# Warm-up products, another order of the first norm, roundings and averages at other places, values in groups of four

## What is computed

```python
x = x + L0(_gn(x))      # q, k, v = g @ W + b; softmax(q k^T / 8 + rel_h + rel_w) v; @ Wp + bp
x = x + L1(_gn(x))      # qkv = g @ qkv_w^T; softmax over 49 neighbours; @ out_w^T

def _gn(v, G=32, eps=1e-5):
    g = v.reshape(B_, H_, W_, G, C_ // G)
    m = jnp.mean(g, axis=(1, 2, 4), keepdims=True)
    s = jnp.var(g, axis=(1, 2, 4), keepdims=True)
    return ((g - m) / jnp.sqrt(s + eps)).reshape(v.shape)
```

## Time and profile before

| | us |
|---|---|
| median of 3 runs | 3250.79 |
| lowest and highest | 3249.35, 3253.89 |
| profiled run, its time | 3253.59 |
| its span in the trace | 3251.8 |
| TensorE busy | 3164.5 (97%) |
| VectorE, ScalarE, GpSimd busy | 1731.7, 1228.9, 1085.2 |

### The profile page before, as it was taken

The page is one execution under the profiler, slowest core; times in us unless marked ns, Lnnn a source line. Parts: engine busy times, 40 slices in busy tenths (PEclk is TensorE's granted clock), DMA queues, the critical chain, the costliest instruction groups (busy, mean ns, idle before and its releaser), DMA issues.

```text
span 3251.8 us, 48955 instructions
## 1 busy us (share of the span) xinstructions
PE 3164.5 (97%) x20428; PEld 2368.3 (73%) x20428; DVE 1731.7 (53%) x1889; ACT 1228.9 (38%) x1397; POOL 1085.2 (33%) x618
## 2 busy tenths in 40 slices
PE   8999999999999999999999999999999999999999
PEld 6876658886787665888678756588877876568876
DVE  4447745346434774543644477444473457744435
ACT  2345542224234554213423455321342346532132
POOL 0037770025003776002400477600340047750043
PEclk9999999999999999999999999999999999999999
DMA  3211013113421101311432100121153111022103
GB/s 124 91 36 24 20 45 117 40 53 121 140 99 27 24 20 48 114 40 59 139 134 80 33 21 17 58 104 44 61 165 116 65 34 27 14 88 81 40 24 123
DMA packets 170520, 220.39 MB, mean 68 GB/s; under 512 B 113856, under 2 KB 126400, under 8 KB 170304
## 3 DMA queue, kind: packets, MB, share of 16 engines
q1 hardware_dynamic: 168768, 215.68, 21.2%
q10 hardware_dynamic: 1536, 1.57, 0.2%
HBM read 141.70 MB, written 50.33 MB: 59 GB/s over the span
## 4 chain that ended last, share of the span: by engine, by line
PE 83%; DVE 5%; issue 4%; ACT 3%; SPq 2%; DMA 2%; POOL 1%; ACTq 0%; DVEq 0%; POOLq 0%
PE score L1156 15%; PE score L1157 14%; PE score L1158 14%; PE lot L1313 10%; PE score L1278 9%; PE lot L1228 5%; PE lot L1231 4%; PE score L1285 3%; PE score L1291 3%; SPq L428 2%; DVE recip L931 2%; PE lot L1330 1%; PE lot L1199 1%; PE lot L1261 1%; PE lot L1156 1%
## 5 line engine op out<-in xcount | busy, mean ns | idle before, releaser
L568 POOL TENSOR_TENSOR acc<-acc,prob 128x1024 f32<-128x1024 f32 x288 | 714.9, 2482 | 240.0 <-ACT prob L748 211.3
L748 ACT ACTIVATE prob<-score 128x1024 f32<-128x1024 f32 (+3 forms) x576 | 512.5, 908 | 374.7 <-PE score L1291 296.2
L889 DVE TENSOR_REDUCE max_part<-lot 128x1 f32<-128x512 f32 x640 | 411.1, 684 | 173.4 <-PE lot L1231 173.4
L1313 PE MATMUL lot<-prob,v 128*64 128x512 f32 (+4 forms) x2496 | 470.9, 514 | 7.2 <-ACT o_raw L647 4.4
L1156 PE MATMUL score<-a_hi,w_hi 128*128 128x512 f32 x1152 | 459.1, 399 | 12.9 <-DVE q_lo L1002 5.1
L1157 PE MATMUL score<-a_lo,w_hi 128*128 128x512 f32 x1152 | 450.8, 391 | 0.0
L1158 PE MATMUL score<-a_hi,w_lo 128*128 128x512 f32 x1152 | 450.0, 391 | 0.0
L568 POOL TENSOR_TENSOR acc<-prob 128x1024 f32<-128x1024 f32 x48 | 113.8, 2372 | 860.9 <-ACT prob L748 860.9
L815 DVE TENSOR_TENSOR w_lo<-raw,w_hi 128x1536 fp32r<-128x1536 f32 x95 | 178.8, 1882 | 298.2 <-ACT w_hi L605 297.9
L1156 PE MATMUL score<-w_hi,a_hi 128*128 128x256 f32 x1152 | 336.1, 292 | 0.0
L1313 PEld LDWEIGHTS lot<-prob,v 128*64 128x64 f32 x2496 | 161.5, 136 | 235.9 <-issue 199.1
(11 more groups left out here) (112 smaller groups left out, 5456.5 us busy)
## 6 DMA issues: line engine op xcount, KB each, us to landing
raw<-weights SPq DMA_DIRECT2D x96, 768.0 KB, 4.4
g_mem<-g SPq DMA_DIRECT2D x24, 1024.0 KB, 4.7
xin<-x_t SPq DMA_DIRECT2D x24, 512.0 KB, 6.0
xr<-x_t SPq DMA_DIRECT2D x24, 512.0 KB, 5.0
x_mem<-xr SPq DMA_DIRECT2D x24, 512.0 KB, 6.5
xr<-x_mem SPq DMA_DIRECT2D x24, 512.0 KB, 5.6
y_t<-xr SPq DMA_DIRECT2D x24, 512.0 KB, 6.8
recip<-recip SPq DMA_DIRECT2D x368, 32.0 KB, 1.9
```

What stands on the lines that cost most here:

```text
L568: nc.gpsimd.tensor_tensor(acc[:, :, a:b], with_, now, ALU.add).then_inc(added, 1)
L748: nc.scalar.activation(prob[:, ug % P_SLOTS, :, 0:b - a], score[:, u % 2, :, 0:b - a], ACT.Exp, scale=SCALE).then_inc(prob_ok, 1)
L889: nc.vector.reduce_max(max_part[:, t, part, h:h + 1], lot[:, (2 * n + h) % 3, :], AX.X)\
L1313: last = nc.tensor.matmul(lot[rows_of(h), bank, x - half * HALF:y - half * HALF], v[:, t, p * 128 + 64 * h:p * 128 + 64 * h + 64], prob[:, ...
```

## The change

TensorE gets six products of `ones` at its start. VectorE does the first part's means ahead of the fourth tile's statistics, its variance ahead of the fifth's and its first norms ahead of the sixth's. In phase 0 the averages of the second part move between the first projections. On ScalarE `bias_first` moves from unit 13 to unit 10 of a layer 0 pair, and the rounding of chunk 9 from unit 5 to unit 9 of its last pair (on VectorE too). In layer 1 the values stand in fours (units 0 to 3 behind the scores of unit 5, units 4 to 7 behind those of unit 1 of the next pair), and `out_copy` goes from unit 1 to unit 2. At the end of layer 1 `shift_averages` goes from behind the first output tile to behind the sums, and `group_variances` behind `invert`.

```diff
@@ -34,6 +34,7 @@
 ADDS = (2 * QT - 2, QT - 2)
 PARTS = (2, 1)
 GROUPED = 4
+WARM_UP = 6
 ORDER = (list(range(QT)), [0, 7, 1, 6, 2, 5, 3, 4])
 P_SLOTS = 6
 LAST = PAIRS - 1
@@ -756,24 +757,24 @@
                                 out_hi(f, p - 1, 0)
                             if u == 5 and ahead:
                                 bias_turn(f, p + 2, 0)
-                            if u in (5, 13) and p == LAST:
-                                weight_hi(f, QK_CHUNKS + V_CHUNKS + u // 8)
+                            if u in (9, 13) and p == LAST:
+                                weight_hi(f, QK_CHUNKS + V_CHUNKS + u // 13)
                             if u == 7 and p:
                                 out_hi(f, p - 1, 1)
                             if u == 9:
                                 if ahead:
                                     bias_turn(f, p + 2, 1)
                                 sums_copy(f, p, 0)
+                            if u == 10 and ahead:
+                                bias_first(f, p + 2)
                             if u == (11 if p else 13) and p < LAST:
                                 widen(f, p + 1)
                             if u == 12:
                                 out_copy(f, p, 0)
                             if u == (12 if p else 13) and p < LAST:
                                 bias_hi(f, p + 1)
-                            if u == 13 and ahead:
-                                bias_first(f, p + 2)
                         else:
-                            if u == 1 and p:
+                            if u == 2 and p:
                                 out_copy(f, p - 1, 0)
                             if u == 3 and p:
                                 sums_copy(f, p - 1, 0)
@@ -953,17 +954,18 @@
                 statistics(0, i)
                 if i == 2:
                     aggregate(0, 0)
+                    group_means(0, 0)
                 if i == 3:
-                    group_means(0, 0)
+                    group_variances(0, 0)
+                if i == 4:
+                    norm(0, 0)
+                    norm(0, 1)
+                    input_lo(0, 0)
             aggregate(0, 1)
-            group_variances(0, 0)
-            norm(0, 0)
-            norm(0, 1)
-            input_lo(0, 0)
-            group_means(0, 1)
             norm(0, 2)
             input_lo(0, 1)
             input_lo(0, 2)
+            group_means(0, 1)
             group_variances(0, 1)
             for i in range(3, CT):
                 norm(0, i)
@@ -1069,8 +1071,8 @@
                             normalise(f, p - 1, 0)
                         if u == 2 and p:
                             invert(f, p - 1, 1)
-                        if u in (5, 13) and p == LAST:
-                            weight_lo(f, QK_CHUNKS + V_CHUNKS + u // 8)
+                        if u in (9, 13) and p == LAST:
+                            weight_lo(f, QK_CHUNKS + V_CHUNKS + u // 13)
                         if u == 5 and p:
                             normalise(f, p - 1, 1)
                         if u == 9 and p:
@@ -1087,8 +1089,9 @@
                 else:
                     if nx < PHASES:
                         group_means(nx, 0)
+                    invert(f, LAST, 0)
+                    if nx < PHASES:
                         group_variances(nx, 0)
-                    invert(f, LAST, 0)
                     normalise(f, LAST - 1, 0)
                     out_lo(f, LAST - 1, 0)
                     normalise(f, LAST, 0)
@@ -1331,9 +1334,14 @@
                 last.then_inc(sum_mm, 1)
                 sums_issued[0] += 1
 
+
+            pe.wait_ge(const_ok, 1)
+            one_column = ones[:, 0:1]
+            for n in range(WARM_UP):
+                nc.tensor.matmul(score[:, 0, 0, :], one_column.to_broadcast([128, 128]),
+                                 one_column.to_broadcast([128, HALF]), start=True, stop=True)
             mean_averages(0, 0)
             shift_averages(0, 0)
-            mean_averages(0, 1)
             for f in range(PHASES):
                 layer = f % 2
 
@@ -1356,9 +1364,9 @@
                         pe.wait_ge(o_ok, (f - 1) * TILES + 8 + 2 * j)
                     for i in range(3):
                         project(j, i)
-                        if f % 2 and j == 0 and i == 1:
+                        if len(norm_parts(f)) > 1 and j == 0 and i == 1:
                             mean_averages(f, 1)
-                        if len(norm_parts(f)) > 1 and j == 0 and i == (2 if f else 0):
+                        if len(norm_parts(f)) > 1 and j == 0 and i == 2:
                             shift_averages(f, 1)
                 for i in range(3, CT):
                     for j in range(2):
@@ -1405,12 +1413,12 @@
                     for u in range(UNITS[layer]):
                         if layer == 1:
                             scores(f, p, u)
-                            if u % 2 and u > 1:
-                                values(f, p, u - 3)
-                                values(f, p, u - 2)
+                            if u == GROUPED + 1:
+                                for e in range(GROUPED):
+                                    values(f, p, e)
                             elif u == 1 and p:
-                                values(f, p - 1, QT - 2)
-                                values(f, p - 1, QT - 1)
+                                for e in range(QT - GROUPED, QT):
+                                    values(f, p - 1, e)
                             if u == 3 and p:
                                 sums(f, p - 1, 0)
                             if u == 5 and p < LAST:
@@ -1437,7 +1445,7 @@
                             sums(f, p - 1, 1)
 
                 last_pair = PAIRS - 1
-                for u in range(UNITS[layer] - (2 if layer else GROUPED), UNITS[layer]):
+                for u in range(UNITS[layer] - GROUPED, UNITS[layer]):
                     values(f, last_pair, u)
 
                 def output(n, c):
@@ -1458,9 +1466,9 @@
                     pe.wait_ge(o_lo_ok, last_part(f, c))
                     for n in range(4):
                         output(n, c)
-                    if early and c == 0:
-                        shift_averages(f + 1, 0)
                 sums(f, last_pair, PARTS[layer] - 1)
+                if early:
+                    shift_averages(f + 1, 0)
                 pe.wait_ge(w_lo_ok, first + 2)
                 pe.wait_ge(out_copied, last_part(f, last_pair))
                 for c in range(2):
```

## The result

The changed kernel takes 3217.03 us (median of 4 runs, 3214.89 to 3221.12), the kernel before 3252.34 us (4 runs, 3249.35 to 3257.75). The ratio is 0.9888 with a 95% interval of 0.9875 to 0.9902, so it is 1.1% faster, 35.3 us. The profiled run is the fastest of the four, 3214.89 us with a span of 3213.1 us, 38.7 us under the span before.

What follows compares the result with a forecast made beforehand. TensorE, busy 97% of the span, bounds the kernel; its waits and half-rate clock stretches can be won. 18.8 + 13.1 + 2.6 + 8.5 - 7 - 2 = 34.0 us off 3250.8 gives 3217 us, range 3200 to 3238.

Steps and rivals of the forecast that it cites:

- the forecast case: Whole kernel: the summed terms hold, 34.0 us gained, median 3217 us; chance 0.50.
- Last pair of layer 0: Chunk 9's rounding moved to unit 9, four times: waits for prob and slow clock go, 18.8 us gained.
- First pair: Layer 0, bias_first moved to unit 10, four times: most of the b_hi wait and slow clock go, 13.1 us gained.
- rival 1: Clock still falls at layer 0's first pair and behind the new shift averages, taking back 9.5 and 4.9 us: 3231; chance 0.22.
- Pairs 1 to 3: Layer 0, same bias_first move, twelve times: 0.61 us wait goes, unit 13's scores come later, 2.6 us gained.
- End of layer 1: Shift averages behind the sums, three times: 3.6 us of waits and 4.9 us of slow clock go, 8.5 us gained.
- Groups of four: Layer 1's values in fours, 24 pairs: fewer visits to the values but more waits for exponentials, 7 us lost.
- The start: Products of ones and new norm order, once: first a_lo earlier, but slow clock and later second variance, 2 us lost.
- both sets of averages (3 us each at that rate): At the start, second part's averages between first projections run at half rate, its variance coming some 6 us later.
- the slower case: Exponentials bound layer 1, six units of each pair paying 0.5 us, 72 us over 24 pairs: 3282; chance 0.05.
- rival 4: TensorE meets other waits at once in the last pair and at layer 1's end, 6 us gained: 3245; chance 0.09.
- Rival 2: Grouping in layer 1 costs nothing and the clock stays up at the start, 14 us better: 3203; chance 0.14.

Runs made afterwards that it cites:

- seam: twos with ScalarE's out_hi and w_hi at layer 1's seams moved, VectorE's out_lo along, and b_lo behind the next reduction in layer 0's first pair: 3204.07 us.
- group_earlier: seam with SyncE's load of group one pair earlier in layer 1, and GpSimd's first w_lo waiting for the squared shift: 3199.70 us.
- w_hi_unit7: The changed kernel, fours kept, with layer 1's w_hi in pairs 4 and 5 behind the exponential of unit 7 instead of unit 6: 3206.98 us.
- no_warm_up: The changed kernel without the six products of ones at TensorE's start: 3217.48 us.
- fill: The changed kernel with more products of ones: seven at the start, one behind the mean averages, five behind the shift averages: 3213.69 us.
- gated_w_lo: The changed kernel without products of ones, GpSimd's first w_lo waiting until VectorE has written the squared shift: 3213.52 us.
- twos: The changed kernel with layer 1's values in twos again and out_copy back at unit 1: 3208.44 us.

## Why the prediction was right, and where it was not

The median came out as forecast, 3217.03 against 3217, and the forecast case is the one that happened. That it fits this closely is luck: the runs of the kernel lie 6 us apart. And the terms were not all right: the profiled run gained 38.7 us where the sum had 34.0. Three terms were too favourable (by 1.0, 1.6 and 1.4 us), three not favourable enough (by 2.3, 3.8 and 6.4 us), and 3.8 us were lost at places that the sum did not have.

**Last pair of layer 0: right.** 17.8 us, alone 17.3, against 18.8. GpSimd was late next, with 0.53 us a time where I had 0.4. The four waits added up to 12.9 us, and 2.1 us came in their place, which leaves 7.0 us for the slow clock where half of its busy time says 7.5.

**First pair: right in its mechanism, 1.6 us too high.** Both waits left over came as worked out, 1.31 + 1.16 us for 1.3 + 1.25. The clock's part was too high, because a stretch at 0.50 in this place runs partly through time that would else be waiting. The changed kernel has one such stretch in the first image (the window from 240.1). The wait of 1.16 us is missing there, and the pair takes 44.56 us, 0.2 more than the others. Where seam and group_earlier leave only 0.43 us of this wait, a stretch costs 0.9 us (44.5 against 43.6). Both come to some 1.3 us of slower products less the wait that they fill. By that, rival 1 with its 9.5 us back here would have been too dear for stretches of this length, even with one in all four pairs; the changed kernel had one in one pair.

**Pairs 1 to 3: 4.9 us instead of 2.6**, 0.41 a time. The new wait at unit 13 came with 0.35 to 0.39 us as foreseen, so 0.61 less 0.38 should leave 0.2. It leaves twice as much, in the kernel with this part alone too (44.1 against 44.5 us). The rest lies in gaps too short for the views, which name waits from 0.15 us on: set side by side, row by row, the starts of pair 2 show 0.12 us at the values that follow unit 13's scores, and 0.07 us at the product that waited for `b_hi`.

**End of layer 1: 12.3 us instead of 8.5.** The failed step is the one that left 3.2 us of the clock's cost in place, because two stretches came behind the small products of the mean averages "which stay". Both are gone in the changed kernel. One of them came behind a wait ahead of these averages, 0.51 us for the load of `group`, which I had not seen; the other behind no such wait, as I had it. Alone, this part brought 10.7 us and kept one such stretch, behind the wait. In the changed kernel the averages of the second image start 1.8 us after the load has landed, and all three ends take 9.80 us. They come that late because of the wait of 1.26 us in the last pair: w_hi_unit7, without it, waits 0.31 us for the load again. And the 9.80 us in all three images are luck in part. Three kernels with the same end, no_warm_up, fill and gated_w_lo, have no wait there either, and still 4 of their 9 ends hold a stretch at 0.50 and take 11.4 us. So what brings the clock down behind these averages is not settled; that two such stretches stay each time was too high.

**Groups of four: 8.4 us lost for 7, and the size was right by other waits than named.** The wait of 1.5 us at the last pair was there, with 1.26 us, 5 of the 8.4 us; with the step moved the pair is 2.0 us shorter, nearly the whole 2.2 us that it loses against twos. Of the waits of 0.39, 0.15 and 0.18 us in each pair only one shows, with 0.21 us, and the pairs 0 to 4 are even with those of twos in sum. The pair came out at 12.45 us, inside the 12.2 to 12.7 named. In the first image 1.7 us more went into a stretch at 0.50 behind the 1.26 us wait.

**The start: wrong in sign, 4.4 us gained for 2 lost.** The first half was right: the averages ended ahead of `w_lo`, `rstd` followed it (15.18 us), the first `a_lo` came at 18.01 for 18.3, and the clock fell again at 11 us. What failed is "both sets of averages (3 us each at that rate)". The clock rose at about 24.7 us, 5 us after the first projection, so both sets ran at 1.62 us. The second part's variance came at 29.68 us, 0.7 us later than before (28.97) and not 6, and the third unit at 43.83 us, where the prediction named 47 as the earliest. Before, products reached the full rate only at 34.9 us, 11.6 us after the first projection, with the shift averages at half rate in between (2.98 us from 25.95 on). I had carried that length over. In no_warm_up the projections begin at 23.16 us, as before (23.25), and the second part's mean averages at 28.54 us already run at 1.62 us. So it is the new order, and not the products of ones, that has the full rate back sooner; why, no run shows.

**What the sum left out.** The late weights in the last image with the slow clock behind them, 3.3 us. The trace of before has no such wait. Three of the later kernels have one like it in one image each: w_hi_unit7 (1.12 us and a stretch), seam (0.76 us and a stretch) and twos (0.53 us). Why a transfer is late in one image of four was not tried, so whether the change makes it more likely is open.

The rivals: apart from 0.21 us a pair, exponentials bound layer 1 nowhere but at `w_hi`, so the slower case had its mechanism in one pair of six instead of all. Waits did take the place of waits (rival 4), between a seventh (0.53 for 3.78 us) and three quarters (2.47 for 3.44 us) of the old length, but most of the clock's part went with the old ones. Rival 2 had the five pairs right and the start in its sign.

## What to carry to other kernels

A wait of a few microseconds on TensorE can be worth nearly double (3.78 us of wait and 2.4 us of slow clock in the last pair of the first image), because the clock may fall behind it: price both, but the clock's part only as far as TensorE would not wait anyway. Before pricing a regrouping, look for the one step (here a 1.5 us rounding) that stands between two exponentials which the new order needs in a row; moving it behind both brought 9 to 10 us. When a wait is removed, read what lands next on all queues, SyncE's loads too: the profile may name such a wait only "issue", and the rows of the other engines must be read beside it.

## What the runs showed of the hardware

- A VectorE step of three columns beside GpSimd's `w_lo` takes as long as that instruction still runs: 2.34 us before, 2.83 us in no_warm_up, 3.33 us in fill, where it came 0.11 us too late. Ahead of it, it takes 0.16 us. Both its inputs are in SBUF; statistics and a variance with an input from TensorE's bank ran beside `w_lo` undisturbed.
- The clock behind one and the same wait does not fall each time. Behind the 1.26 us of the last pair of layer 1 it fell in 8 of 16 cases (the changed kernel, no_warm_up, fill and gated_w_lo, four images each; 17.1 us for the pair instead of 15.46). Each fall costs 1.7 us, so such chances spread the runs of a kernel by some microseconds, and a gain of 3 us at one place is seen in the trace and not in a median of four or five.
- A wait named "issue" ahead of products had a cause both times it was followed up: the load of the tile that the products read (seam, 1.96 us; the products start 0.2 us after it lands), and a result of VectorE held up by a late transfer (the changed kernel, 1.69 us).
- A stretch at 0.50 costs less where it covers a wait: 0.2 us in the first pair of layer 0 where it takes the place of a wait of 1.16 us, 0.9 us where it takes the place of one of 0.43 us.
